# Gates folded into the delta rule's u and w, and a convolution that reads PSUM, in an eight-sequence hybrid model with a redrawn order

## What is computed

```
def _short_conv(x, w):
    K = w.shape[1]
    L = x.shape[1]
    xp = jnp.pad(x, ((0, 0), (K - 1, 0), (0, 0)))
    return sum((xp[:, j:j + L, :] * w[:, j] for j in range(K)))
...
q = jax.nn.silu(_short_conv(x @ Wq, conv_q)).reshape(B, L, H, dk)
k = jax.nn.silu(_short_conv(x @ Wk, conv_k)).reshape(B, L, H, dk)
v = jax.nn.silu(_short_conv(x @ Wv, conv_v)).reshape(B, L, H, dv)
...
u = T @ v_c
wm = T @ kb_c
...
def step(S, xs):
    q_i, k_i, u_i, w_i, wm_i = xs
    u_i = (u_i - wm_i @ S) * w_i[..., None]
    a = jnp.where(causal, q_i @ jnp.swapaxes(k_i, -1, -2), 0.0)
    o_i = q_i @ S + a @ u_i
    return (S + jnp.swapaxes(k_i, -1, -2) @ u_i, o_i)
...
o_l = _delta_scan(cd(qh), cd(kh), cd(vh * bl[..., None]), cd(kh * bl[..., None]), c1(wl))
o_g = _delta_scan(cd(qh), cd(kh), cd(vh * bg2[..., None]), cd(kh * bg2[..., None]), c1(wg))
```

## Time and profile before

| | |
|---|---|
| median of three runs | 1290.52 us (1286.07 to 1291.62) |
| the profiled execution | 1297.51 us, its span 1295.0 us |
| granted TensorE clock, mean | 0.979 |
| TensorE matmul / weight load busy | 91% / 72% |
| VectorE, GpSimd, ScalarE busy | 75%, 66%, 56% |
| DMA | 230.87 MB, mean 178 GB/s |

### The profile page before, as it was taken

How to read it: one execution, slowest core, us unless ns; L and a number is a source line. 1 busy time by engine, 2 the same in 40 slices (tenths; PEclk the granted TensorE clock), 3 DMA queues, 4 the chain that set the end, 5 groups by cost and what they waited for, 6 DMA issues and landing times.

```text
span 1295.0 us, 31167 instructions
## 1 busy us (share of the span) xinstructions
PE 1175.6 (91%) x11890; PEld 930.8 (72%) x11890; DVE 971.2 (75%) x1950; ACT 721.9 (56%) x2060; POOL 851.1 (66%) x1157
## 2 busy tenths in 40 slices
PE   5778799899999798899999999989999898989898
PEld 3455477777678677777778777877688776878686
DVE  5858799876995969877687977968768956865354
ACT  5787876458655562567456665437666533332322
POOL 3746466686787727787568754887639876865841
PEclk9999989999999999999999999999999999999999
DMA  6111165555376438764566563775348565767673
GB/s 255 34 38 34 37 237 191 167 192 163 100 242 207 139 105 264 233 200 130 178 205 210 153 193 124 265 243 171 101 135 262 185 220 183 268 223 250 222 249 125
DMA packets 91186, 230.87 MB, mean 178 GB/s; under 512 B 9888, under 2 KB 16160, under 8 KB 90912
## 3 DMA queue, kind: packets, MB, share of 16 engines
q1 hardware_dynamic: 90896, 228.30, 54.3%
q10 hardware_dynamic: 144, 0.59, 0.1%
HBM read 225.71 MB, written 3.15 MB: 177 GB/s over the span
## 4 chain that ended last, share of the span: by engine, by line
PE 32%; DVE 24%; ACT 5%; DMA 4%; issue 3%; POOL 0%; DVEq 0%; ACTq 0%; POOLq 0%
PE bank L899 8%; PE bank L946 6%; DVE ogate L1352 5%; PE bank L827 3%; PE bank L936 2%; DVE dy L1210 2%; DVE kv L1123 2%; DMA kv<-values 2%; PE bank L612 2%; PE bank L917 1%; PE bank L927 1%; DVE mmin L1341 1%; PE bank L647 1%; DMA ogate<-gates 1%; PE bank L671 1%
## 5 line engine op out<-in xcount | busy, mean ns | idle before, releaser
L1748 POOL TENSOR_TENSOR vgate<-vgate,xT 128x512 f32<-128x512 f32 x256 | 330.3, 1313 | 102.4 <-DMA vgate<-gates 102.1
L899 PE MATMUL bank<-wv,vgate 128*128 128x128 f32 x2048 | 257.5, 280 | 6.4 <-DVE prob L1055 2.4
L899 PEld LDWEIGHTS bank<-wv,vgate 128*128 128x128 f32 x2048 | 245.3, 194 | 17.4 <-issue 5.2
L946 PE MATMUL bank<-ogate,wo 128*128 128x256 f32 x1024 | 244.4, 385 | 7.7 <-DVE ogate L1352 6.7
L946 PEld LDWEIGHTS bank<-ogate,wo 128*128 128x128 f32 x1024 | 189.8, 191 | 40.6 <-issue 14.3
L1352 DVE TENSOR_TENSOR ogate<-ogate,bank 128x1024 f32<-128x1024 f32 x128 | 152.9, 1212 | 33.3 <-PE bank L936 30.3
L1463 ACT ACTIVATE prob<-prob,mx 128x128 f32<-128x128 f32 (+1 forms) x256 | 96.0, 377 | 53.7 <-DVE mx L1059 53.4
L1681 POOL TENSOR_TENSOR rot<-rot 128x512 f32<-128x512 f32 x64 | 81.6, 1275 | 56.6 <-DVE rot L1035 56.2
L1630 ACT ACTIVATE mprob<-bank,mmin 128x256 f32<-128x256 f32 x128 | 59.2, 468 | 104.3 <-DVE mmin L1341 104.1
L1724 POOL TENSOR_TENSOR step<-dlt,uw 128x126 f32<-128x126 f32 (+22 forms) x248 | 92.5, 373 | 24.7 <-DVE dlt L1275 8.7
L1726 POOL TENSOR_TENSOR dlt<-dlt,step 128x126 f32<-128x126 f32 (+22 forms) x248 | 95.4, 385 | 19.4
(11 more groups left out here) (227 smaller groups left out, 2493.1 us busy)
## 6 DMA issues: line engine op xcount, KB each, us to landing
vgate<-gates SPq DMA_DIRECT2D x128, 512.0 KB, 4.5
ogate<-gates SPq DMA_DIRECT2D x128, 512.0 KB, 4.2
wv<-in_wv_moe SPq DMA_DIRECT2D x128, 256.0 KB, 4.8
wo<-in_wo_moe SPq DMA_DIRECT2D x128, 256.0 KB, 4.6
kv<-values SPq DMA_DIRECT2D x64, 256.0 KB, 4.5
local<-in_local SPq DMA_DIRECT2D x1, 1715.0 KB, 10.6
wqkv<-in_wqkv SPq DMA_DIRECT2D x2, 768.0 KB, 7.0
x<-in_x SPq DMA_DIRECT2D x8, 128.0 KB, 5.3
```

What stands on the lines that cost most here:

```text
L899: i = nc.tensor.matmul(out[:, n * D:(n + 1) * D], xg[:, e, n * P:(n + 1) * P], m.wv[slot][:, e, :], start=(q, n, e) == (0, 0, 0), stop=(q, ...
L946: i = nc.tensor.matmul(out[:, 0:T], m.wo[slot][:, e, :], cg[:, e, :], start=(h, q, e) == (0, 0, 0), stop=(h, q, e) == (MH - 1, 1, EQ - 1))
L1748: i = tt(gate[:, e:e + half, :], gate[:, e:e + half, :], spread(m.xT[b % 2][:, :], 1, half), ALU.mult)
```

## The change

Four edits, and all six order strings drawn anew.

1. The gates are multiplied into u and w once, as VectorE reads them out of PSUM (a new `uw` on VectorE, two 128x512 multiplies per batch), in place of ScalarE's copy. In the chunk loop the multiply L1296 goes, and with it `s.du`; `ds` on TensorE and `du` on GpSimd wait for the subtraction alone.
2. `conv` reads the projection where `din` left it. The taps are applied newest first: the first multiply covers all 256 columns, and each multiply-add shifts by one more column (255, 254, 253). `pad`, its zeros and ScalarE's three copies go.
3. `din` puts q and k in one bank and v in another: two banks in place of three. They are released by `conv`.
4. The tables of the order and of the banks.

```diff
-         "fT": 1, "fsel": 1, "din": 3, "l2": 1, ...
+         "fT": 1, "fsel": 1, "din": 2, "l2": 1, ...
...
     def din(b):
-        for k in range(3):
-            bank = banks.of("din", b, i=k)
+        for i, kinds in enumerate(((0, 1), (2,))):
+            bank = banks.of("din", b, i=i)
             out = take(bank)
             x_ready(b)
-            nc.tensor.matmul(out[:, 0:T], m.w_delta[:, k, :], m.xT[b % 2][:, :], start=True, stop=True).then_inc(bank.filled, 1)
+            for at, k in enumerate(kinds):
+                last = nc.tensor.matmul(out[:, at * T:(at + 1) * T], m.w_delta[:, k, :], m.xT[b % 2][:, :], start=True, stop=True)
+            last.then_inc(bank.filled, 1)
...
     def ds(b, c):
-        bank = banks.of("ds", b, c)
+        bank, new = banks.of("ds", b, c), banks.of("du", b, c)
         out = take(bank)
-        pe.wait_ge(s.du, nth("du", b, c))
+        pe.wait_ge(new.emptied, new.use)
...
     def conv(b, k):
-        raw = banks.of("din", b, i=k)
-        v.wait_ge(raw.emptied, raw.use)
-        v.wait_ge(s.zeroed1, 1)
+        bank = banks.of("din", b, i=k // 2)
+        raw, out = filled(bank)[:, k % 2 * T:(k % 2 + 1) * T], m.dy[b % 2][:, k, :]
...
-        v.chain(ts(m.dy[b % 2][:, k, :], m.pad[:, k, 0:T], m.conv[:, k, 0:1], None, ALU.mult))
-        for j in range(1, CONV):
+        v.chain(ts(out, raw, m.conv[:, k, CONV - 1:CONV], None, ALU.mult))
+        for late in range(1, CONV):
             v.settle()
-            i = stt(m.dy[b % 2][:, k, :], m.pad[:, k, j:j + T], m.conv[:, k, j:j + 1], m.dy[b % 2][:, k, :], ALU.mult, ALU.add)
+            i = stt(out[:, late:], raw[:, 0:T - late], m.conv[:, k, CONV - 1 - late:CONV - late], out[:, late:], ALU.mult, ALU.add)
...
+    def uw(b, half):
+        bank = banks.of("uw", b, half)
+        v.wait_ge(s.dw, nth("dgates", b))
+        rows = m.uw[:, half * NC_:(half + 1) * NC_, :, :].rearrange("p c a t -> p c (a t)")
+        tt(rows, chunks(filled(bank)), spread(m.gates[b % 2][:, 2 + half, :], 2, 2 * CH), ALU.mult).then_inc(bank.emptied, 1)
...
     def du(b, c):
...
         tt(m.dlt[:, c, :, :], u4[:, c, :, :], out, ALU.subtract).then_inc(bank.emptied, 1)
-        v.wait_ge(bank.emptied, bank.use)
-        tt(m.dlt[:, c, :, :], m.dlt[:, c, :, :], spread(m.gates[b % 2][:, 2:4, c], 2, CH), ALU.mult).then_inc(s.du, 1)
...
-            act(m.pad[:, k, CONV - 1:], filled(bank)[:, 0:T], ACT.Copy).then_inc(bank.emptied, 1)
...
-    def uw(b, half):
-        bank = banks.of("uw", b, half)
-        act(m.uw[:, half * NC_:(half + 1) * NC_, :, :], filled(bank).rearrange("p (c a t) -> p c a t", c=NC_, a=2),
-            ACT.Copy).then_inc(bank.emptied, 1)
```

More of the change, by code:

```diff
@@ new lines @@
+GPSIMD_TURNS = (
+    "aaaaaaaaGbGbGbGabaGaaGGaGaababGabaabaaaababbGGbGGGaGaaaGaGaababGbaaaaaaabaWWWbbGGWWaaWWaaGGWbWabaaaWbWbGGbGWWb"
+    "WDWDGDDDWWDaDWWaaDaDaGaabbaDDDDbaDDaGaDDWWaGDDbDaGDDaWGDaWaGWDbGWbGWWDGbDDDDDWWDaWWaaaDWaabaaDGWDWbDDbWDGDGGbD"
+    "DDbDGDDWDDDDWWWWWDDDDDWWDaaaDaWDWaaaaDGbWbWaaGaabWaDbaaDaGGDWDDWWbDbDDWDWDDDDGDbDbWWDaaDaDGDGGGWaaWDGGWWGaGDDa"
+    "aDGWDbWbWWbaWaaabDDDDDaDDWWWbbDaDDDaWDDaWDDWWbbDWWDWGDDWDWGGGWDWDWGaaaWDaGaDaGGaabWbWDWDbDDbDaDaDaDaDDWDaDaDDb"
+    "WGbDaaDbWbDDaaaDaDaWWDWaDaaWWDbDbWWGGGWGWbbWDDDDDWWDGWDGDDWWWGDGWDDDWDDWWGWDWWDDDDDDDWWDWWWDDWDDDDDDWDDDDWDDDW"
+    "WDWDDDDDDDDWWWDDWWDWDDDWDWDDDDDDDD")
@@ L329 @@
          "hnT": 1, "ff": 3, "w2": 1, "end0": 1, "gk": 1, "gqk": 1, "gz": 1, "gv": 1, "gg": 1, "grms": 1, "gadd": 1,
-         "fT": 1, "fsel": 1, "din": 3, "l2": 1, "dgate": 1, "kk": 1, "uw": 1, "du": 1, "ds": 1,
+         "fT": 1, "fsel": 1, "din": 2, "l2": 1, "dgate": 1, "kk": 1, "uw": 1, "du": 1, "ds": 1,
          "gsend": 1, "fuse": 2, "mqk": 1, "mpT": 1, "mend": 1}
@@ L1206, in conv @@
             v.wait_ge(read.filled, read.fill)
-        v.chain(ts(m.dy[b % 2][:, k, :], m.pad[:, k, 0:T], m.conv[:, k, 0:1], None, ALU.mult))
-        for j in range(1, CONV):
+        v.chain(ts(out, raw, m.conv[:, k, CONV - 1:CONV], None, ALU.mult))
+        for late in range(1, CONV):
             v.settle()
-            i = stt(m.dy[b % 2][:, k, :], m.pad[:, k, j:j + T], m.conv[:, k, j:j + 1], m.dy[b % 2][:, k, :], ALU.mult, ALU.add)
-            if j < CONV - 1:
+            i = stt(out[:, late:], raw[:, 0:T - late], m.conv[:, k, CONV - 1 - late:CONV - late], out[:, late:], ALU.mult, ALU.add)
+            if late < CONV - 1 or k == 0:
                 v.chain(i)
-        i.then_inc(s.conv, 1)
+            else:
+                i.then_inc(bank.emptied, 1)
     def y(b):
@@ L1570, in fsel @@
         sigmoid(m.lp[:, :, :], m.lg[:, :, :], s.lp_raw)
-    def din(b):
-        for k in range(3):
-            bank = banks.of("din", b, i=k)
-            act(m.pad[:, k, CONV - 1:], filled(bank)[:, 0:T], ACT.Copy).then_inc(bank.emptied, 1)
     def silu(b):
-        a.wait_ge(s.conv, nth("conv", b, 2))
+        for i in range(2):
+            bank = banks.of("din", b, i=i)
+            a.wait_ge(bank.emptied, bank.use)
         sigmoid(m.de[:, :, :], m.dy[b % 2][:, :, :], s.silu)
@@ L1732, in du @@
     def du(b, c):
-        g.wait_ge(s.du, nth("du", b, c))
+        new = banks.of("du", b, c)
+        g.wait_ge(new.emptied, new.use)
         tt(m.dlt_sum[:, c, :], m.dlt[:, c, 0, :], m.dlt[:, c, 1, :], ALU.add).then_inc(s.dus, 1)
```

113 lines of the change are left out of this document (52 added, 61 removed).

## The result

The changed kernel takes **1239.24 us** (median of four runs, 1233.68 to 1240.69) against 1291.07 (1286.07 to 1293.31) for the kernel before beside it: ratio 0.9596, 95% interval 0.9555 to 0.9637. That is 52 us or 4.0% faster; the forecast was 1282, with a range down to 1266. The profiled execution took 1239.64 us, its span is 1238.2 us (before 1297.51 and 1295.0).

The account below looks back on a forecast made before the run. TensorE, busiest at 91%, was taken as the bound, with at most 75.8 us idle to win. On-chain terms netted 16.7 us; half, 8.4, off the 1290.5 median gave 1282 us, likeliest range 1276 to 1288, overall 1266 to 1300.

Parts of the forecast that it names:

- The prices of single instructions: VectorE: multiply-adds from the bank 481 ns, first convolution multiplies 480, new gate multiplies 680; VectorE work falls 43.1 us.
- The sum: Whole kernel: on-chain savings less the new multiplies net 16.7 us; half of that, 8.4 us, was taken as the gain.
- the ceiling: Whole kernel: 16.7 us, the net on-chain saving, as the most to win; 2.7 us if only TensorE's idle share counts.
- on-chain share: Time the last-ending chain lay on changed lines: gates 9.7, multiply-adds 8.5, first multiplies 1.4, ScalarE 0.9, less 3.8 us.
- ScalarE's copies: Dropping 24 + 16 copies takes 18.7 us off ScalarE, 56% busy and hidden by slack; worth 0.9 us on the chain.
- The order: Redrawn tables on all engines: not priceable from the trace; bounded at about 10 us, gained or lost.
- TensorE's work the same 1175 us: Sign in the changed profile: TensorE's busy time stays at 1175 us.
- Its idle after 162 us about 67: Sign in the changed profile: TensorE's idle time after 162 us about 67 us, where it was 75.8.
- Rival 1: Hidden anyway: freed VectorE time becomes idle time; 1288 us, 1285 to 1292; chance 0.19.
- rival 3: Bank does not end the convolution's hold-up, so the gates alone gain 3 us: 1287 us; chance 0.05.
- Rival 2: Two longer-held din banks stall TensorE, 18 us over eight batches: 1300 us, slower; chance 0.13.
- Rival 4: All of the chain's 16.7 us, plus up to 10 from waits the new order removes: 1274 to 1264 us; chance 0.17.

Follow-up runs that it names:

- e7: Changed kernel, but ScalarE still makes its three copies per batch to pad and the convolution, reading the banks, waits for them: 1255.43 us, ratio 0.9745.
- e9: Changed kernel with no gate multiply anywhere and ScalarE copying u and w out of PSUM (gates left out of the result): 1253.38 us, ratio 0.9739.
- e1: All old code in the new order, against the kernel before: 1301.22 us, ratio 1.0102.
- e4: Kernel before, in its old order, with the gates edit alone: 1282.93 us, ratio 0.9965.
- e15: Kernel before without the 64 gate multiplies and their wait, ScalarE still copying u and w (gates left out of the result): 1280.98 us, ratio 0.9935.
- e11: Kernel before with GpSimd's vgate in four instructions of 128x256 in place of two of 128x512: 1268.70 us, ratio 0.9848.
- e2: Changed kernel with the gates edit alone undone: 64 multiplies back in the chunk loop, 16 copies back on ScalarE: 1263.14 us, ratio 0.9819.
- e6: Changed kernel with gates multiplied in the chunk loop, reading the subtraction's result in the bank, and ScalarE's u and w copies back: 1259.83 us, ratio 0.9776.
- e3: Changed kernel with the convolution edit alone undone: ScalarE copies to pad and VectorE reads SBUF: 1275.46 us, ratio 0.9904.
- e10: Changed kernel with GpSimd's vgate in four instructions of 128x256 in place of two of 128x512: 1248.36 us, ratio 0.9691.
- e12: Changed kernel with a 128x64 copy from the bank added on VectorE ahead of each of the 72 multiply-adds: 1253.17 us, ratio 0.9732.

## Why the prediction was wrong

*The prices of single instructions: right.* Multiply-adds 482 ns (forecast 480), first multiplies 473 (480), `uw` 686 (680), ScalarE 707.2 us (703). The convolution's 19.8 and 3.3 us of VectorE work and the gates' 31.0 - 10.8 came out as priced. VectorE's remaining 14 us of the 57.5 are hold-ups of lines that the change doesn't touch, `lc`, `xn`, `lsel` and others, which fell otherwise in the new order (a few others rose, `do` by 3.1 us).

On the rule of the Trainium skill, VectorE: DVE Perf Modes (rules for kernel authors), which for many operations on a product names the copy from PSUM to SBUF first, and otherwise to accept the slower mode: the copy did not pay in this case, 482 ns from the bank against a mean of 756 from SBUF, and 16 us for the copy itself in e7, at its turns there. The rule that fits is on another page, SBUF — State Buffer, Who interferes with whom: a VectorE instruction with two SBUF inputs contends with a GpSimd instruction that reads SBUF, and one with at most one such input, outside the two-port modes, doesn't. The trace agrees, 479 to 485 ns in all 72 cases with one input in the bank, 50 of them beside a GpSimd instruction.

*The sum: wrong, and this is the step that failed.* "Between 2.7 and 16.7 I take half of the ceiling, 8.4 us". The on-chain share was no ceiling. In the new order the gates are worth 24 us where the sum had 9.7 - 3.8 = 5.9 as its most, the convolution 36 where it had 8.5 + 1.4 and part of 0.9. The share tells how long the last-ending chain lay on a line; it leaves out what is queued behind the line on engines that work strictly in order (`mqk` behind the silu, `mprob` behind the copies), and the clock after the stall. It also covers the span from 405 us on alone; stretched to all 1133 us after 162 it would make 16.7 x 1133 / 890 = 21 us, still far from 60.

*"ScalarE's copies", "what hides them is that slack": wrong.* e7 puts 16 us on the 24 copies, and e9, with the 16 others and less VectorE work, lies 14 us above the change. The forecast looked at ScalarE's 56% busy time and at who waits for the copy (0.6 us in e7). It left out what the copy waits for: ScalarE, in strict order, stands for TensorE's product, and all behind it comes late. Both prices hold for the turns that I gave the copies, not for copies as such.

*"The order", "about 10 us, gained or lost": wrong in kind.* The new order alone *loses* 13 us (e1 against 1288.0, with the old stages at turns chosen by hand). With the new code it gives 52. The order isn't a term beside the others: what it is worth depends on the instructions that it arranges. The old order for its part won only 5 us from the gates edit (e4) and 9 from a loop without gates (e15), where the forecast's sum gives 3 to 5.9 and 5 to 9.7. So for the gates the reckoning came out, or nearly so, under the old order, and failed with an order drawn anew; the convolution alone was not run in the old order. Nor does it hold for every edit there: e11 takes 28.9 us off VectorE, which at VectorE's part of the chain (24 of 68) makes 10.2 us at most, and wins 21.

*"TensorE's work the same 1175 us": wrong*, 1161.1; at most 8.6 of the 14.5 us are the clock's. "Its idle after 162 us about 67": 37.2.

*The rivals.* Rival 1 (hidden anyway) and rival 3 (the hold-up stays) are refuted by 52 us and by 479 to 485 ns. Rival 2 (banks stall): in the changed kernel no wait of L707 for `dy` is to be found; it costs nothing there, as forecast. Rival 4 had the right direction, all of the chain's share and a better order, but 26 us were its most, and the order alone is not better (e1).

*What stays open.* Why an order that suits its instructions gives so much isn't resolved further: I could not draw an order of my own for the old code, so how far the old kernel would come with one is unknown; e11 says it had at least 21 us left in it. The simplest test is missing too: e2, e7 and e9 with ScalarE's copies a turn or two later. How much of the 24 and the 36 us is the edits' own, and how much the turns' of the stages that were put back, is therefore open.

## What to carry to other kernels

Where all engines follow one fixed order, don't price an edit by the on-chain share of its line: follow what is queued behind the line on every in-order engine, and treat code and order as one change, since either alone may win little or lose (1283 with the gates alone, 1301 with the order alone) where both together win (1239). A copy on an engine with slack is not free, so ask what it waits for and what is queued behind it. Put a stage that waits behind those that are ready. If VectorE works beside a GpSimd that reads SBUF, leave one of its two operands in PSUM.

## What the runs showed of the hardware

- The hold-up of VectorE by GpSimd was seen on fp32 operations with all operands in SBUF: a 128x256 multiply-add of 483 ns takes up to 1567; with one operand in a bank it never passes 485. With a bank nothing of it is left. The gate multiply shows the same: 224 to 1318 ns from SBUF, 224 to 226 in all 64 cases of e6, where one operand is in a bank.
- Halving the GpSimd instruction doesn't halve the longest hold-up: with `vgate` at a median of 731 ns in place of one of twice the size, the longest multiply-add was still 1565 ns and the median rose to 828, while the mean fell from 756 to 709. The rows of e11, single instructions:

```profile
L1748 POOL TENSOR_TENSOR vgate<-vgate,xT x512: 717/731/1637, 169.6 to 1243.4; 128x256 f32<-128x256 f32 x171
```

```profile
L1210 DVE SCALAR_TENSOR_TENSOR dy<-pad,layer,dy x72: 483/828/1565, 162.0 to 1106.2; 128x256 f32<-128x256 f32 x72
```

- Behind a stall of 4.98 us the four products of L919 took 2.05 us, against 1.10 without it, at a granted clock of 0.50 and 1.00, the two levels of 1.2 and 2.4 GHz. The eight kernels one step from the changed one (e2, e3, e6 to e10, e12) lose 23.8 to 30.4 us to the clock in their profiles, and the changed one 18.6. By the medians of all runs it is 23.1 to 29.4 against 20.4, so for e10, the lowest, the difference is not clear.
